# Another order of scores and value segments in a head pair of a fused attention and expert layer

## The reference, cut to what matters

```python
def _L0_attn_ref(x, Wq, bq, Wk, bk, Wv, bv, Wo, bo):
    ...
    scores = jnp.einsum('bqhd,bkhd->bhqk', Q, K) * scale
    scores = scores + _alibi_bias(S, H, x.dtype)[None]
    attn = jax.nn.softmax(scores, axis=-1)
    out = jnp.einsum('bhqk,bkhd->bqhd', attn, V).reshape(B, S, D)
    return out @ Wo + bo
...
xn = _layernorm(x, axis=-1)
x = x + _L0_attn_ref(xn, ...) + _L0_ffn_ref(xn, ...)
```

## Time and profile before

| what | before |
|---|---|
| device time, median of 3 runs | 2350.14 us (2348.15 to 2351.96) |
| device time of the profiled execution | 2350.06 us |
| its span, first to last instruction | 2348.2 us |
| PE busy | 2314.1 us (99%) |
| VectorE busy | 1969.0 us (84%) |
| ScalarE busy | 1747.4 us (74%) |
| copies of a pair's result (L938), first and last | 219.3 and 1413.2 us |

### The profile page before, as it was taken

One profiled execution on the slowest core, in us unless ns is written; L12 is line 12 of the kernel. 1 busy time (PEld: TensorE's weight loads), 2 busy tenths in 40 slices (PEclk: granted clock), 3 DMA queues, 4 the chain that ended last, 5 costly groups with the idle time before them and its releaser, 6 DMA issues.

```text
span 2348.2 us, 51054 instructions
## 1 busy us (share of the span) xinstructions
PE 2314.1 (99%) x19358; PEld 1521.6 (65%) x19358; DVE 1969.0 (84%) x3154; ACT 1747.4 (74%) x3400; POOL 1179.7 (50%) x1442
## 2 busy tenths in 40 slices
PE   7999999999999999999999999999999999999998
PEld 6875444444444444444444439999999989888998
DVE  7888999999999999999999967777777765555555
ACT  4447999999999999999999997777777753333332
POOL 2114667764446666666666523343333344455444
PEclk9999999999999999999999999999999999999999
DMA  8995544442224333333333315777777754455443
GB/s 293 376 342 175 159 140 150 149 131 81 70 75 125 98 116 111 101 114 103 106 116 99 109 56 197 244 237 244 235 246 233 247 164 136 128 151 147 141 134 104
DMA packets 172597, 374.71 MB, mean 160 GB/s; under 512 B 41108, under 2 KB 87700, under 8 KB 159140
## 3 DMA queue, kind: packets, MB, share of 16 engines
q1 hardware_dynamic: 134384, 210.78, 27.8%
q0 software_dynamic: 36880, 159.87, 21.3%
q10 hardware_dynamic: 1088, 0.79, 0.1%
HBM read 240.00 MB, written 140.31 MB: 162 GB/s over the span
## 4 chain that ended last, share of the span: by engine, by line
PE 92%; DVE 5%; ACT 2%; issue 1%; DMA 1%; SPq 0%; POOL 0%; DVEq 0%; ACTq 0%; POOLq 0%
PE ps L610 89%; PE ps L623 3%; DVE mx L1103 2%; DVE mx L1106 1%; ACT ptb L930 0%; ACT pta L930 0%; ACT qkH L910 0%; DMA xr<-Xn 0%; DMA OPS<-Md 0%; DMA xt<-in_x 0%; DVE qkL L1091 0%; POOL rstd L1343 0%; DVE xn L1075 0%; DVE stats L1035 0%; DVE WB0c L1228 0%
## 5 line engine op out<-in xcount | busy, mean ns | idle before, releaser
L1103 DVE TENSOR_REDUCE mx<-ps 128x1 f32<-128x512 f32 x1304 | 819.5, 681 | 16.4 <-PE ps L610 14.3
L610 PE MATMUL ps<-OPS 54*128 54x512 f32 (+1 forms) x4096 | 737.3, 447 | 3.8 <-DVE mx L1106 2.1
L610 PEld LDWEIGHTS ps<-OPS 54*128 54x128 f32 (+1 forms) x4096 | 351.0, 184 | 503.0 <-ACT pta L930 203.0
L930 ACT ACTIVATE pta<-ps 128x512 f32<-128x512 f32 x1024 | 545.3, 617 | 42.2 <-PE ps L610 32.0
L930 ACT ACTIVATE ptb<-ps 128x512 f32<-128x512 f32 x1024 | 549.0, 621 | 30.9 <-PE ps L610 26.8
L610 PE MATMUL ps<-OPS,WB 128*128 128x256 f32 (+2 forms) x2364 | 384.9, 315 | 2.9 <-DVE VB L1245 1.5
L1106 DVE TENSOR_REDUCE mx<-ps 128x2 f32<-128x1024 f32 x310 | 377.8, 1219 | 8.1 <-PE ps L610 5.1
L610 PEld LDWEIGHTS ps<-OPS,WB 128*128 128x128 f32 (+1 forms) x2364 | 332.9, 183 | 27.8 <-issue 3.3
L610 PE MATMUL ps<-ptb,VB 128*32 128x256 f32 (+2 forms) x4040 | 311.6, 392 | 0.0
L610 PE MATMUL ps<-pta,VB 128*32 128x320 f32 (+2 forms) x3544 | 284.8, 420 | 0.1
L610 PE MATMUL ps<-OPS,WB0c 128*128 128x256 f32 (+2 forms) x1248 | 206.3, 317 | 1.3 <-ACT accs L938 0.9
(11 more groups left out here) (176 smaller groups left out, 3159.5 us busy)
## 6 DMA issues: line engine op xcount, KB each, us to landing
OPS<-QKh SPq DMA_DIRECT2D x512, 64.0 KB
Xs<-zero POOLq DMA_DIRECT2D x71, 256.0 KB, 2.8
xr<-Xs SPq DMA_DIRECT2D x71, 256.0 KB, 5.2
Ys<-VB SPq DMA_DIRECT2D x71, 256.0 KB, 5.0
QKh<-qkH SPq DMA_DIRECT2D x16, 1024.0 KB, 6.9
QKl<-qkL SPq DMA_DIRECT2D x16, 1024.0 KB, 8.6
OPS<-QKl SPq DMA_DIRECT2D x256, 64.0 KB
OTd<-accs SPq DMA_DIRECT2D x64, 256.0 KB, 2.2
```

What stands on the lines that cost most here:

```text
L610: return self.e.matmul(o, l, r, start=start, stop=stop)
L930: self.e.activation(pt(m)[:, half * GT:(half + 1) * GT], ps[:, score_bank(n), :], ACT.Exp).then_inc(sem["exp"], 1)
L1103: self.e.reduce_max(mx[:, r % 2, hh, i, half:half + 1], ps[:, bank, :], AX.X).then_inc(sem["mxred"], 1)
```

## The change

It changes five tables of numbers and letters. The strings of `PAIR` now have twelve `P` in place of eleven; `WIDTHS` has twelve segments, of the same sum (4096 columns), and its first three still make 1024. `DOUBLE` names units 16/17, 20/21, 24/25 and 28/29 in place of 2/3, 10/11, 18/19, 24/25 and 28/29; `COPIED` names units 1 and 9 in place of 4 and 8.

```diff
 PAIR = (
-    "SuSuSuPSuSuSuPSuSuP",
-    "SuSuSuPSuSuSuPSuSuT",
-    "SuPSuSuSuPSuSuSuPSu",
-    "SuSuPSuSuSuPSuSuSuP",
+    "SuSuPSuSuPSuSuSuPSu",
+    "SuSuPSuSuSuPSuSuSuPT",
+    "SuSuSuPSuSuPSuSuPSu",
+    "SuSuPSuSuPSuSuSuPSu",
 )
...
-WIDTHS = 512, 224, 288, 480, 544, 256, 416, 288, 288, 480, 320
+WIDTHS = 256, 256, 512, 448, 480, 320, 288, 288, 224, 256, 256, 512
...
-DOUBLE = (1, 5, 9, 12, 14)
-COPIED = (4, 8)
+DOUBLE = (8, 10, 12, 14)
+COPIED = (1, 9)
```

## The result

The changed kernel takes 2357.32 us, median of 11 runs (2354.65 to 2360.72), beside 2350.03 of the kernel before on the same chip (11 runs, 2348.15 to 2352.33). The ratio is 1.0029, with a 95% interval of 1.0021 to 1.0036: slower by 7.3 us, where I had forecast faster by 8.6. The profiled execution took 2356.31 us, with a span of 2354.5.

What follows compares the result with a forecast made beforehand. PE was taken to set the pace, VectorE having 2% of room. A pair was to take 18.52 + 0.19 of stalls = 18.71 us for 18.90; 43 pairs x 0.20 = 8.6 us off 2350.06 gave 2341.5, range 2336 to 2353.

Steps and rivals of the forecast that it cites:

- The other waits: In a pair, result copy, finish, transpose, segments and exponentials wait for nothing more in the new order: no cost.
- What bounds, and the price of a segment and a run: In attention's pairs PE sets the pace; one more segment with the same columns costs a certain 0.38 us a pair.
- estimate from two pages of the Trainium skill: The added segment costs 0.11 us where rows say 0.39; a pair 0.28 shorter, the whole 12 us faster than forecast.
- The stalls of the new order: PE's late loads in runs six, seven and ten: 0.03 + 0.12 + 0.04 = 0.19 us a pair, for 0.77 before.
- Singles for doubles: VectorE's work rises from 18.49 to 18.55 us a pair, costing nothing while PE needs 18.71.
- the first 18 pairs: Early pairs, 19.39 us each on VectorE's added work: no gain counted; five or so gain 0.2, others lose up to 0.06.
- VectorE keeps its idle time: Rival: bursts of PE keep VectorE idle as before, a pair 18.9 to 18.96, 2350 to 2352 us; chance 0.14.
- The doubles hold banks too long: Rival: VectorE's doubles at units 28/29 and 20/21 stop PE, 0.38 us a pair, 7 us slower, 2357; chance 0.13.
- No stalls are left: Rival: exponentials come a tenth earlier, a pair takes 18.52, 16 us faster, 2334; chance 0.07.
- The sum: Whole kernel: 43 pairs x 0.20 = 8.6 us gained, 2350.06 - 8.6 = 2341.5 us.

Runs made afterwards that it cites:

- one_direct: Kernel after with only the second of a pair's four indirect transfers made plain, into a tensor of its own: 2343.15 us, 0.9971 of the kernel before.
- after_early: Kernel after with the second indirect transfer of a pair issued at key chunk 1, behind the first: 2343.91 us, 0.9972 of the kernel before.
- after_gate_b: Kernel after with the second indirect transfer waiting until score 16 is done, run once more on another chip: 2343.39 us, 0.9970 of the kernel before.
- after_direct: Kernel after with all 128 indirect transfers made plain ones to fixed places, rows not sorted by expert: 2343.10 us, 0.9969 of the kernel before.
- early_three: Kernel after with the second indirect transfer issued early and units 28 and 29 as singles, three doubles for four: 2343.77 us, 0.9979 of the kernel before.
- after_gate: Kernel after with the second indirect transfer in its place but waiting until score 16 is done: 2343.51 us, 0.9975 of the kernel before.
- old_doubles: Kernel after with the doubles of before (1, 5, 9, 12, 14): 2391.76 us, 1.0182 of the kernel before.
- old_copies: Kernel after with the copied units of before (4, 8): 2356.12 us, 1.0031 of the kernel before.
- before_again: The kernel before, unchanged, run and profiled again: 2350.04 us, ratio 0.9999.

## Why the prediction was wrong

The step that failed is the one headed **The other waits**, which ended in "nothing". It went through the waits that the program writes between PE, ScalarE and VectorE, and left out GpSimd's indirect transfers, which stand in the order of the very pairs that I timed. In its place the runs show 0.5 us in each of 21 pairs, 11.2 us in all, in which ScalarE waits for PE's signal of score 16 during the second transfer; with that one transfer plain (one_direct) or moved (after_early, after_gate_b) it is gone. Point by point:

- **What bounds, and the price of a segment and a run: right.** In the pair at 737 us runs of 4 take 0.67 where nothing holds them (743.97 to 744.64) and a segment of 288 takes 0.62 (744.64 to 745.26, formula 0.63). By the prediction's estimate from two pages of the Trainium skill ("TensorEngine Tiling (Array Packing)", section Key Properties, and "TensorE: Matmul & The Clock Gate", section Step-by-step: what each phase is for) a pair would take 18.43; the shortest after the change took 18.75 (after_direct).
- **The stalls of the new order: right in kind, short in size.** An undisturbed pair takes 18.79 (732.39 to 751.18) for the 18.71 forecast. Its runs take 10.26 together, where bare runs are 9.92: stalls of 0.34 for 0.19, of which segments 0.07 shorter than the formula give some back. The three runs that I had late are late: the sixth by 0.05 (forecast 0.03), the seventh by 0.07 (0.12), the tenth by 0.05 (0.04). Two more are: the ninth by 0.07 (0.75), and the fourth, scores 7 to 9, by 0.12 (1.02). At the fourth a double holds units 28/29. I had given it 0.06 of room from a start as soon as its second tile was there; VectorE started it 0.12 later than that. In early_three, where this double is two singles, that run takes 0.90. Over 43 pairs 0.08 is 3.4 us: with the transfer out of the way the change gives 0.25 to 0.31% (after_early, after_gate, after_direct, one_direct), 6 to 7 us, where I had 8.6.

The same pair of the kernel after, PE first: the first run, the tenth, and the next pair's first. Then VectorE at the double of the fourth run.

```profile
732.39 0.97 PE L610 MATMUL ps<-OPS 54*128 54x512 f32 x6
...
746.53 1.02 PE L610 MATMUL ps<-OPS 54*128 54x512 f32 x6
747.48 0.64 PE L610 MATMUL ps<-pta,VB 128*32 128x256 f32 x8
...
751.18 0.98 PE L610 MATMUL ps<-OPS 54*128 54x512 f32 x6
```

```profile
736.03 1.22 DVE L1106 TENSOR_REDUCE mx<-ps 128x2 f32<-128x1024 f32 x1
```

- **Singles for doubles, and the first 18 pairs: right.** VectorE is busy 98.0% of the stretch (797.49 of 813.47) and not over 99% as I had written, since the slow pairs leave it idle: in after_direct, without them, it is 99.0%. The first 18 pairs are 0.25 us shorter together.
- **VectorE keeps its idle time: no.** Its waits for PE fell from 2.9 to 0.6 us in 13 pairs.
- **The doubles hold banks too long:** its 2357 came out by luck. Its mechanism is there in small, the 0.12 at units 28/29, but the fast pairs have it too and take 18.78. A rival that ends at the measured time has proved nothing; one_direct, in which no double moves, takes all of the loss away.
- **No stalls are left: no.**
- **The sum.** 43 pairs at 18.78 would be 807.5 us for 813.5, a gain of 6.0. The 21 pairs with a held signal add 11.2, and the other 22 together 0.2. The net of this is the 5.4 measured.

Half a microsecond in a pair is long for one signal, because the order can't absorb it: score 16's exponential is the one that frees the bank of score 19, the first load of the next run, and runs of 4 follow, in which the exponentials must catch up. The trace shows it as three late starts in a row (the two PE fences above).

The range, 2336 to 2353, took in no case of this kind. What would have shown it beforehand is one row of GpSimd over a pair, beside the ends of the scores in the new order: a transfer at a fixed distance behind the fold, and score 16, with no copy ahead of it, 0.8 us behind its start. Even then the half microsecond couldn't be read from the profile of the kernel before, where no signal is late.

What stays open is why a signal is held during an indirect transfer, and when. The profiles fall into two kinds. If only gaps over 0.5 us are counted, the profile before, after_gate, early_three, old_doubles and old_copies have none in 128 transfers, and the nine others with all four indirect have 48 to 80. The last four of those without any are all the profiles of one chip; on each of the three other chips every profile with indirect transfers has them. So the stretches may belong to the chip. The kernel after wasn't run on the chip without them, where it may be as fast as after_gate; for the first two profiles the chip isn't on record. The record of updates differs too: the trace of before holds 41101 and that of before_again, the same kernel, 36639, so in part a silent stretch is a lack of records. Why 20 to 23 of the 31 pairs from 27 to 57 are hit is open as well: in the profile after, score 16 ends 0.79 to 0.86 us after the transfer's start in the late pairs and 0.79 to 0.83 in the others, so the times in the trace don't tell them apart.

## What to carry to other kernels

When an order is changed, lay every instruction of every engine's queue in the stretch beside the new order, GpSimd's transfers too, and ask which waiting engine is now idle at a moment when it had work in hand before. An instruction that costs nothing (here a copy on ScalarE, as I read the rows) may hide something that the profile of before can't show. And look at pairs one by one before believing their mean: 18.78 and 19.3 are two different cases, and the mean of them looked like a small stall everywhere. The version that beats both kernels is the changed order with the one transfer behind score 16, or well ahead of it: 2343.4 us, 0.9970 [0.9960, 0.9981] (after_gate_b), and 2343.9, 0.9972 [0.9962, 0.9982] (after_early).

## What the hardware showed that I had not expected

- An indirect transfer of 128 rows issued by GpSimd (1.04 to 1.13 us each) can delay another engine's semaphore signal: in 11 of the 16 profiles with such transfers there are stretches without a recorded update from about 0.65 to 1.3 us after its start, and a ScalarE that waits idle for PE's signal there starts 0.5 us late (20 to 23 times in each of four profiles). I saw it for PE's signals to ScalarE alone.
- A plain transfer of the same rows doesn't. It takes some 0.6 us on GpSimd (128 of them in after_direct), and moves the same packets and bytes in the same kind of queue. Page, part 3, of the kernel after and then of after_direct (queue: packets, MB, share of the engines' span):

```profile
q0 software_dynamic: 36880, 159.87, 21.0%
```

```profile
q0 software_dynamic: 36880, 159.87, 21.1%
```

- The page "DMA: Bandwidth & Descriptors" of the Trainium skill, section SWDGE vs HWDGE vs iDMA, says that GpSimd writes the descriptors of its transfers by software, direct and indirect ones alike. By these runs that can't be the whole reason, since 0 of 128 plain ones show a silent stretch and the loss is gone with them. What is special to the indirect ones I have not tried.
- A silent stretch costs nothing where the engines have work in hand: 83 of them in one_direct and 76 in before_again cost no time that can be measured.
